# A four-layer graph network: a piece of the last quarter's adjacency matrix is turned and widened earlier

## What is computed

```python
def _L2_gnn_ref(h, adj_mat, W, a):
    N = h.shape[0]
    ht = (h @ W).reshape(N, N_HEADS, N_HIDDEN).transpose(1, 0, 2)
    src = jnp.einsum('hnd,hd->hn', ht, a[:, :N_HIDDEN, 0])
    dst = jnp.einsum('hnd,hd->hn', ht, a[:, N_HIDDEN:, 0])
    e = jax.nn.leaky_relu(src[:, :, None] + dst[:, None, :], SLOPE) + adj_mat[None]
    att = jax.nn.softmax(e, axis=-1)
    h_prime = jnp.einsum('hij,hjd->hid', att, ht)
    return h_prime.mean(axis=0)

h = jnp.maximum(_layernorm(x, axis=-1), 0.0)
x = x + _L2_gnn_ref(h, adj, L2_gnn_W, L2_gnn_a)
```

## Time and profile before

| | us |
|---|---|
| median of 3 runs | 706.86 |
| lowest and highest | 706.56 and 707.75 |
| profiled execution, time | 707.33 |
| profiled execution, span from first to last instruction | 705.5 |
| attention's steps on PE | from about 290 to 640 of the span |

### The profile page before, as it was taken

One profiled execution on the slowest core, in us unless ns is written; L12 is line 12 of the kernel. 1 busy time (PEld: TensorE's weight loads), 2 busy tenths in 40 slices (PEclk: granted clock), 3 DMA queues, 4 the chain that ended last, 5 costly groups with the idle time before them and its releaser, 6 DMA issues.

```text
span 705.5 us, 15958 instructions
## 1 busy us (share of the span) xinstructions
PE 684.2 (97%) x6413; PEld 584.9 (83%) x6413; DVE 620.8 (88%) x1148; ACT 459.4 (65%) x798; POOL 111.5 (16%) x146
## 2 busy tenths in 40 slices
PE   3989999999999999999999999999999899999998
PEld 3876888888888974488888888888888788888887
DVE  7888999958898968899999999999999799994672
ACT  3987057638888328975559676587866678655650
POOL 3005722321123210011100021100211000000000
PEclk9998999999999999999999999999999999999999
DMA  9996999993799977779988799988999894464391
GB/s 334 378 336 258 424 426 308 303 230 123 219 271 252 208 189 191 192 180 246 214 189 248 143 222 249 232 236 175 203 235 239 222 199 78 83 191 139 130 311 38
DMA packets 169016, 159.53 MB, mean 226 GB/s; under 512 B 115760, under 2 KB 128752, under 8 KB 164720
## 3 DMA queue, kind: packets, MB, share of 16 engines
q1 hardware_dynamic: 147584, 100.32, 52.8%
q0 software_dynamic: 19056, 41.42, 26.2%
q10 hardware_dynamic: 2304, 16.78, 5.7%
HBM read 69.86 MB, written 52.46 MB: 173 GB/s over the span
## 4 chain that ended last, share of the span: by engine, by line
PE 88%; DVE 4%; ACT 4%; issue 3%; POOL 0%; ACTq 0%; POOLq 0%
PE ps L839 16%; PE ps L841 16%; PE ps L840 16%; PE ps L777 6%; PE ps L885 4%; PE ps L886 4%; PE ps L675 3%; PE ps L677 3%; PE ps L676 3%; PE ps L724 3%; PE ps L726 3%; PE ps L725 3%; DVE arena L1253 2%; PE ps L704 2%; DVE arena L1339 1%
## 5 line engine op out<-in xcount | busy, mean ns | idle before, releaser
L839 PE MATMUL ps<-arena 128*128 128x257 f16 x1024 | 279.9, 273 | 1.9 <-DVE arena L1477 1.9
L841 PE MATMUL ps<-arena 128*128 128x257 f16 x1024 | 279.4, 273 | 0.0
L840 PE MATMUL ps<-arena 128*128 128x257 f16 x1024 | 279.2, 273 | 0.0
L1169 ACT ACTIVATE arena<-arena 128x512 f16<-128x512 f32 x252 | 158.4, 628 | 98.0 <-PE ps L841 77.6
L1470 DVE SCALAR_TENSOR_TENSOR arena<-arena,w_j 128x512 f32<-128x512 f32 x256 | 190.0, 743 | 0.0
L1477 DVE TENSOR_TENSOR arena<-arena 128x512 f16<-128x512 f32 x256 | 175.7, 687 | 9.6 <-ACT arena L1169 9.3
L839 PEld LDWEIGHTS ps<-arena 128*128 128x128 f16 x1024 | 99.9, 98 | 14.8 <-ACT arena L1169 2.1
L840 PEld LDWEIGHTS ps<-arena 128*128 128x128 f16 x1024 | 100.3, 98 | 12.6
L841 PEld LDWEIGHTS ps<-arena 128*128 128x128 f16 x1024 | 99.8, 97 | 13.0
L724 PE MATMUL ps<-arena 128*128 128x257 f16 x256 | 70.3, 275 | 0.0
L726 PE MATMUL ps<-arena 128*128 128x257 f16 x256 | 69.7, 272 | 0.0
(11 more groups left out here) (149 smaller groups left out, 1068.0 us busy)
## 6 DMA issues: line engine op xcount, KB each, us to landing
adj_t<-arena POOLq DMA_DIRECT2D x32, 1024.0 KB, 7.9
arena<-in_adj_dram SPq DMA_DIRECT2D x32, 512.0 KB, 6.2
arena<-in_adj_dram SPq DMA_DIRECT2D x16, 1024.0 KB, 6.1
adj_parts<-arena ACTq DMA_DIRECT2D x16, 1024.0 KB, 22.1
arena<-adj_t SPq DMA_DIRECT2D x64, 256.0 KB, 4.9
arena<-adj_t SPq DMA_DIRECT2D x10, 1024.0 KB, 6.7
x<-arena POOLq DMA_DIRECT2D x15, 512.0 KB, 6.2
arena<-u_rows SPq DMA_DIRECT2D x4, 1024.0 KB, 14.7
```

Of the source, the lines that this page charges most:

```text
L839: mm(ps[:, bank, 0:DE], hi, ht_hi[:, head, j, 0:DE], start=s, stop=False)
L840: mm(ps[:, bank, 0:DE], hi, ht_lo[:, head, j, 0:DE], start=False, stop=False)
L841: ins = mm(ps[:, bank, 0:DE], lo, ht_hi[:, head, j, 0:DE], start=False, stop=e)
L1169: nc.scalar.activation(p_hi[:, j % 4, :], prob[:, j % 4, :], copy).then_inc(p_hi_done, 1)
```

## The change

Two tables of order are changed. No operation is added, removed or resized.

1. The two turns of adj group 12, the first group of the last quarter, no longer stand behind the reload of the third quarter. They stand inside it, between its load groups 1 and 2 (the second and the third of four).
2. On POOL, group 12 is widened behind the addition of head 6 and not of head 7, group 13 behind that of head 7 and not 8, and groups 14 and 15 both behind head 8; before, 15 came behind head 9.

```diff
-        WIDEN_AFTER = {0: (6,), 1: (7,), 3: (8,), 4: (9, 10), 5: (11,), 7: (12,), 8: (13, 14), 9: (15,)}
+        WIDEN_AFTER = {0: (6,), 1: (7,), 3: (8,), 4: (9, 10), 5: (11,), 6: (12,), 7: (13,), 8: (14, 15)}
@@ load_e(q), behind the four loads of group g
                                      ).then_inc(e_loaded[g], 16)
+                    if q == NQ - 2 and g == 1:
+                        for part in range(2):
+                            turn_adj(QB * (NQ - 1), part)
@@ SP, the loop over the quarters
             for q in range(1, NQ):
-                for g in range(TG):
+                for g in range(1 if q == NQ - 1 else 0, TG):
                     for part in range(2):
                         turn_adj(QB * q + g, part)
                 load_e(q)
```

## The result

The changed kernel took **720.17 us** (median of 4 runs, 711.00 to 722.41) against 706.71 us before (4 runs). By the medians it is slower by 13.5 us, or 1.9%. The ratio is 1.0135, with a 95% interval of 1.0086 to 1.0184; it is taken over the runs that count as fast, without the one of 722.41 us, and so is not the quotient of the two medians. The forecast was 707.3, in a range from 705.1 to 709.5, so the result lies far outside it; slower by over 0.2% (1.4 us) had a chance of 0.28. The profiled execution took 719.86 us with a span of 718.0, against 707.33 and 705.5 before.

What follows compares the result with a forecast made beforehand. The prediction took PE to bound the kernel, with 88% of the chain that ended last. Its terms, -1.9 us at the last quarter and +2.4 at the third, made +0.5 on 706.86: 707.3 us, range 705.1 to 709.5.

Steps and rivals of the forecast that it cites:

- The gain: Before the last quarter: earlier widening removes all of PE's wait there, 1.9 us.
- The old stall: Before the last quarter: PE idle 1.86 us, ACT 4.31 us, for the last reload's late second load group.
- One sign of it: In the profile after, POOL's last widening is issued by 526.
- Step 1: Third quarter's reload: the second load group's fourth load lands after 7.2 us, at 464.3.
- step 2: Third quarter's reload: the first turn, issued at 457.5, holds SP until 464.5, between 464.2 and 465.8.
- step 4: Third quarter's reload: third load group takes 6.7 us from first issue to last landing, down at 473.4 (472.5 to 477.2).
- step 5: Third quarter's start: ACT's exponent may start as late as 470.96 at no cost; later, PE loses 2.4 us.
- Step 3: Third quarter's reload: second turn holds SP 1.72 to 2.82 us; third load group starts at 466.7 (465.9 to 468.6).
- the loss: Third quarter's start: PE loses 2.4 us to the late third load group, with bounds of 1.5 to 6.2.
- held longer: Rival, third quarter's reload: first turn holds SP until the addition lands, 465.8; PE loses 4.3 us, 709.3; chance 0.21.
- The other rivals: Loads slip through, only the gain stays, 705.0, chance 0.16; old stall stays, 709.3, or fourth load group late, 0.07.
- The rule on the ring order: SP's queue: a ring is consumed in order, so loads let both turns pass, 707.3; were it not ordered, 705.0.

Runs made afterwards that it cites:

- e3_no_add6: The changed kernel with head 6's addition to x cut to 8 of its 1024 columns; 707.82 us, ratio 1.0007.
- e5_add6_late: The changed kernel, computation complete, with POOL holding head 6's addition until both turns of group 12 have landed; 706.56 us, ratio 0.9980.
- e8_turn_g2: The changed kernel with the two turns one place later, between the third and fourth load group; 706.63 us, ratio 0.9992.
- e4_wait_add6: The changed kernel with SP waiting for head 6's addition to land before it issues the two turns; 713.11 us, ratio 1.0098.
- e10_after_again: The changed kernel once more, unaltered, for the spread and a second trace; 721.85 us, ratio 1.0216.
- e6_add6_copy: The changed kernel with head 6's transfer overwriting x in SBUF instead of adding to it; 710.45 us.
- e7_add6_dram: The changed kernel with head 6's result copied to a spare tensor in DRAM instead of added to x; 710.05 us.

## Why the prediction was wrong

**The gain: right in kind, too large in size.** The old stall came from the widening of group 15 beside the loads; with the new table it is gone, in the changed kernel and in both runs of the table alone. The term was 1.9 us from one execution. A second trace of the kernel before has 1.0, and the medians give 0.6 to 1.0, with intervals that include none. One sign of it failed: the last widening was to be issued by 526, and with the table alone it was at 526.8 and 525.8; in the changed kernel, late by the clash, at 540.6. It was down at 548.5, before the last reload's second group was issued at 556.1.

**Step 1, step 2, step 4 and the rule of step 5: right.** In the changed kernel's trace load group 1 was down at 463.0 (forecast 464.3). The first turn held SP until 463.55, where the forecast had 464.5; in the second trace it was 466.7, above the bound of 465.8. Load group 2 took 476.76 to 482.9 from first issue to last landing, 6.1 us for 6.7. The exponent started at 482.92, and 482.92 - 470.96 = 12.0 us is what the rule of step 5 gives for PE's loss; it was 11.7.

**Step 3 failed.** It took 1.72 to 2.82 us for the time that the second turn holds SP, from turns beside which no accumulating transfer was in flight, and it was 13.07. The third load group was issued at 476.8 and not at 466.7, and that is why PE waited 11.7 us and not 2.4. With that clash removed the step holds: `e3_no_add6` and `e5_add6_late` have 3.05 and 2.77, issue the group at 466.2 and 466.1 (forecast 466.7) and have it down at 473.1 and 472.2 (forecast 473.4). They took 707.8 and 706.6, where 707.3 was forecast. That the times come so near is partly luck: PE waited 1.4 and 0.2 us at that place and not 2.4, so the loss was put too high as well as the gain, and the two errors have opposite signs.

**The rival that was nearest** ("held longer") named the right partner and let it cost 2 us (4.3 instead of 2.4). It took the addition's landing at 465.8 as given, from the trace before, although the addition was a party to the meeting. Here each of the two made the other late. The row that spoke for trouble was there: the addition and the first turn are issued within 0.1 us of each other (457.44 in the earlier trace rows and the end of load group 1 at 457.48 in the earlier trace rows). The other rivals did not come: in the changed kernel nothing waited for the fourth load group, and the old stall is gone.

**The clock** was in no term. PE lost 2.6 us by it behind the wait.

**The rule on the ring order** was hardly put to the test. In no trace did a load of group 2 land before the second turn, but what made the group late came earlier: SP was held for 13.07 us and issued it only at 476.76, when the first turn was about to land. So the delay sat in the issue and not in the ring, and the time to issue was not small beside the transfer's 15.2 us. The Trainium skill, page DMA: Bandwidth & Descriptors, section Rules for kernel authors, says of the pairing of transfers that a transpose next to ordinary DMAs needs nothing. It speaks of what becomes of the data and not of the time, and it doesn't say whether an accumulating transfer counts as ordinary. For the time, the trace shows a cost where the neighbour accumulates: SP is held for 13.07 us instead of 2.77 and 3.05.

**The account of which transfers clash stays partly open.** Turns and accumulating transfers also stand close together in the kernel before, without such a loss: its turns from 300 to 525 us land after 9.4 us at the most. What tells the bad meetings from the harmless ones was not settled. The moment of issue, 0.04 us apart here, is a candidate that no run was made for. The second meetings, of head 7's addition, fit it loosely. Against it stand two meetings of a turn with the accumulating half of a widening, 0.5 us apart in `e8_turn_g2` (16.8 us for the turn) and 0.7 us apart in `e5_add6_late` (issued at 325.91, 15.2 us), while the same meeting in the trace before (326.01 and 326.62) cost the turn 7.6 us. So spacing alone doesn't decide it, and the clash isn't confined to the moved turns; it may also stand behind the longest times of the kernel before, up to 713.1 us, but those have no trace. What the engines do in these 10 us stays open as well.

## What to carry to other kernels

Before a DMA transpose is moved, list not only what is queued behind it but what other queues issue at the same moment, and keep accumulating transfers out of that moment: by place, or by a wait on the one that nobody is in a hurry for (`e5_add6_late`), which cost nothing here, where the wait on the urgent queue (`e4_wait_add6`) cost 6 us. If an edit has two halves, run each alone: here one half held all of the gain and the other all of the loss. And when one transfer's time is taken from the old trace as a bound for another, ask whether the new neighbour leaves that time as it was.

## What the runs showed of the hardware

- A DMA transpose of 512 KB and an accumulating transfer of 512 KB, issued within 0.1 us of each other, held each other up for some 10 us: 19.4 and 19.3 us to landing instead of about 8 each (8.3 in `e5_add6_late`, 8.4 before the change), at 49 GB/s with nearly all engines counted as busy. The same transfer without the accumulation landed in 7.2 us, into SBUF, and 7.0 us, into DRAM; the first transpose beside it took 10.3 and 10.1 us. With the accumulation into DRAM it was 13.0 us.
- Such a meeting is not always bad: a transpose and an accumulating transfer of 1024 KB issued 0.6 us apart landed after 7.6 and 8.7 us in one trace (before, 326.01), and 0.7 us apart after 15.2 and 17.4 us in another (`e5_add6_late`, 325.91).
- A DMA transpose behind loads in its queue held SP until about when these had landed (4.7 to 6.8 us in nine traces, until 0.1 us before to 0.8 us after; in `e10_after_again` 8.9 us, 3.4 us after); with nothing ahead in the queue it held SP for 2.02 us (`e4_wait_add6`).
- PE's granted clock fell to 0.50 during its wait of 11.7 us, and PE worked 5.2 us at it, for a loss of 2.6 us. Behind the waits of 1.4 us in `e3_no_add6` and 3.6 us in `e6_add6_copy` it stayed at 1.00; behind those of 3.1 us in `e7_add6_dram` and 5.8 us in `e4_wait_add6` it fell to 0.50. So a wait of PE of a few us can cost more than its own length, and its length alone doesn't tell whether it does.
